# Row-limited scores and a two-queue first stack in the narrow attentions of a four-layer decoder

## The chip, the cores and the metric

The kernel runs on one core of a Trainium2 chip. The metric is the device time of one execution in microseconds, the median of several runs. The profile is of one execution of its own.

## The reference

The input `x` is (4, 512, 128), the context (4, 154, 128). Four layers follow one another, each with a self part, a cross-attention and a feed-forward part, each with its residual and layer norm. What matters here are the six attentions with 16 heads of 8 dimensions, called narrow below: two self-attentions (L0a, L3a) and four cross-attentions over the 154 context rows (L0x, L1x, L2x, L3x; L1x and L3x have masks). Cut to its core, each computes

```
q, k, v = x @ Wq + bq, src @ Wk + bk, src @ Wv + bv       # split into 16 heads of 8
scores  = einsum('bhqd,bhkd->bhqk', q, k) * scale         # the scale is 1 in L0x
y       = softmax(scores) @ v                             # over k, then heads side by side
x       = layernorm(x + y @ Wo + bo)
```

In L0a the source is rotated by cosines and sines first, in L3a it is projected down first. Everything is float32.

## The kernel before

`build` (L3109) runs the stages one after another, each in a block of its own with a barrier behind it: L0a, L0x, a gated feed-forward, four scans (`mamba`), L1x, a mixture of experts, an attention with shared keys, L2x, a convolution with experts, L3a, L3x, a routed feed-forward. Self-attentions are `self_attention` (L203), cross-attentions `cross_attention` (L701). The feed-forward weights of a coming stage are loaded into the tile `stream` by SyncE just ahead of L0x and of L3x.

**Scores with nine terms.** Float32 scores are made of bf16 matmuls. `split_parts` (L193) splits q and k into PARTS = 3 bf16 parts each, with four operations: `qp` and `kp`, 128 rows (64 for each half of eight heads, dimension by head). All nine products of a part of q with a part of k are summed by one matmul whose contraction runs over TERMS * DH = 72 rows (ROWS) of `qs` and `ks`: nine blocks of eight rows. Behind them are PARTS = 3 rows for the parts of the row maxima in `qs`, against ones in `ks`, so that the turned scores (keys on the rows) come out with the maximum subtracted. The matmuls take all 128 rows of both tiles; so `ks` is filled with ones from row 64 on (GpSimd, L482 or L990) and `qs` with zeros (VectorE L537, or VectorE L1046 and GpSimd L991), once a stage. In L0a and L3a `ks` lies in `stream`.

**How the rows come about.** Eight heads at a time (a "half", n = 0 to 7 for four batches). `stack_q` (L651) moves the three parts of q with three transfers into rows 0 to 23 of `qs`; each takes 64 rows of 512 and puts them into 8 rows of 8 x 512. `stack_k` (L661) does so for k. `turn_q` (L668) waits until q's stacks have landed and copies these rows, cyclically shifted, into rows 24 to 71 with four transfers; `turn_k` (L678) copies k's 24 rows twice, unshifted. All of it is issued by SyncE, in this order, and only the semaphore `turned_...` of the six copies releases TensorE. In the cross-attentions these are L1211 to L1245, and k's rows have 154 columns.

**The order of the work** is written out by hand. Each engine walks over steps J from FIRST to LAST, and constants (Q_AT, K_AT, STACK_AT, TURN_AT, ...) say at which J a batch's or a half's piece of work stands. A step holds four matmuls of turned scores (L321, L834), four of scores (L302; in the crosses four pairs, L807) for heads that lie LEAD steps ahead, and the weighing of the values (L335, L850). VectorE reduces every score tile to its maxima (L542, L1052) and ScalarE takes the exponentials (L405, L917). Scores start at J = -LEAD; what comes before is projecting q and k of the first batch (L279, L284; L779, L784), ScalarE's copies of them (L428, L437; L938, L947), the splits of the first batch on VectorE, and the rows of half 0. The splits of the later batches are GpSimd's. `pad_v` (L557, L1067) clears the value tile once a stage: in the self-attentions VectorE does it before the splits of the first batch, in the crosses already behind them. A half is eight heads, so eight steps J of a self-attention and four of a cross-attention. SyncE also issues the rows of maxima (`put_maxima`), in one order with the stacks and copies.

Of the kernel before, what the change touches and what calls it, by code (L numbers as in the profile page):

```python
# [202 lines left out]
def self_attention(k, name, scale, biased=True):  # L203
# [14 lines left out]
    HALVES = 3  # L218
# [13 lines left out]
    with ExitStack() as ctx:  # L232
# [23 lines left out]
        with phase(k, "chain", "pool_chain", "q_proj", "k_proj", "v_proj", "q_sb", "k_sb", "v_sb", "first_parts",  # L256
                   "q_parts", "k_parts", "q_stacked", "k_stacked", "turned_0", "turned_1", "turned_2", "q_cleared", "k_cleared",
                   "src_proj", "src_cos", "src_sin", "src_ready", "scores", "maxed", "split", "mt_ready", "mt_sb", "mt_row_0", "mt_row_1",
                   "scoresT", "exped", "weighed", "z_out", "zt_ready", "zn_ready", "znT_ready", "znT_sb", "y_ready",
                   "y_read", "var_ready", "eps_added", "rstd_ready", "x_ready", "xT_ready", "xT_sb") as (block, s):  # L260
            @block.tensor
            def _(pe):
# [50 lines left out]
                def scores_turned(J, a):  # L313
# [84 lines left out]
            def _(act):  # L398
# [58 lines left out]

                for J in range(FIRST, LAST):
                    for a in range(G):
# [19 lines left out]
            def _(pool):  # L479
# [24 lines left out]
                def q_parts(b, first):  # L504
                    if first:
                        pool.wait_ge(s["q_sb"], b + 1)

                        pool.wait_ge(s["q_stacked"], 16 * PARTS * 2 * b)
# [4 lines left out]
                def k_parts(b):  # L513
                    pool.wait_ge(s["k_sb"], b + 1)
                    pool.wait_ge(s["k_stacked"], 16 * PARTS * 2 * b)
# [18 lines left out]
            def _(dve):  # L534
                chain = Chain(dve, s["chain"])
                for n in range(HALVES):
                    dve.memset(qs[64:P, n].rearrange("p h t -> p (h t)").bitcast(F32), 0.0).then_inc(s["q_cleared"], 1)  # L537
# [77 lines left out]
                for J in range(FIRST, LAST):  # L615
# [6 lines left out]
                    if batch_at(J, Q_AT) == 0:  # L622
                        pad_v()
# [18 lines left out]
            def _(sp):  # L642
# [44 lines left out]
                for J in range(FIRST, LAST):  # L687
                    if group_at(J, TURN_AT + 1) is not None:
                        put_maxima(group_at(J, TURN_AT + 1))
                    if half_at(J, STACK_AT) is not None:  # L690
                        stack_q(half_at(J, STACK_AT))
                    if half_at(J, STACK_AT + 1) is not None:
                        stack_k(half_at(J, STACK_AT + 1))
                    if half_at(J, STACK_AT + 3) is not None:
                        turn_q(half_at(J, STACK_AT + 3))
                    if half_at(J, STACK_AT + 4) is not None:
# [4 lines left out]
def cross_attention(k, name, scale, biased=True, masks=None, scrambled=False):  # L701
# [12 lines left out]
    TURNED, HALF_UNITS = 6 * 16, G * PER_BATCH // 2  # L714
# [14 lines left out]
    with ExitStack() as ctx:  # L729
# [32 lines left out]
        with phase(k, "chain", "pool_chain", "q_proj", "k_proj", "v_proj", "q_sb", "k_sb", "v_sb", "first_parts",  # L762
                   "q_parts", "k_parts", "q_stacked", "k_stacked", "turned_0", "turned_1", "turned_2", "turned_3", "q_cleared", "k_cleared",
                   "masks_in", "mask_q", "mask_k", "scores", "maxed", "split", "mt_ready", "mt_sb", "mt_row_0", "mt_row_1",
                   "scoresT", "exped", "weighed", "z_out", "zt_ready", "zn_ready", "znT_ready", "znT_sb", "y_ready",
                   "biased", "y_read", "var_ready", "eps_added", "rstd_ready", "x_ready", "xT_ready", "xT_sb") as (block, s):
            @block.tensor
            def _(pe):
# [25 lines left out]
                def scores(J, a):  # L794
                    hh, u, i = 2 * (J + LEAD) + a // 2, a % 2, 4 * (J + LEAD) + a
                    b, h = hh // H, hh % H
                    if h % HH == 0 and u == 0:
                        n = hh // HH
                        pe.wait_ge(s[f"turned_{n % 4}"], TURNED * (n // 4 + 1))
# [5 lines left out]
                    for p in range(2):  # L805
                        qt = 2 * u + p
                        last = pe.matmul(ps[:, i % S_RING, 256 * p:256 * p + CTX], qs[:, b % 2, h, qt * P:(qt + 1) * P],  # L807
                                         ks[:, b % 2, h, :], start=p == 0, stop=not masks, skip_group_check=True)
# [14 lines left out]
                def scores_turned(J, a):  # L823
# [10 lines left out]
                    last = pe.matmul(out, ks[:, b % 2, h, t * KV:(t + 1) * KV], qs[:, b % 2, h, :], start=True, stop=not masks)  # L834
# [75 lines left out]
            def _(act):  # L910
# [56 lines left out]

                for J in range(FIRST, LAST):
                    for a in range(G):
# [17 lines left out]
            def _(pool):  # L987
# [3 lines left out]
                pool.memset(qs[64:P, 1].rearrange("p h t -> p (h t)").bitcast(F32), 0.0).then_inc(s["q_cleared"], 1)  # L991
                pool.wait_ge(s["k_cleared"], 2)
                pool.wait_ge(s["q_cleared"], 2)
# [8 lines left out]
                def q_parts(b, first):  # L1002
                    if first:
                        pool.wait_ge(s["q_sb"], b + 1)
                        if b >= 2:

                            for n in range(2 * b - 4, 2 * b - 2):
                                pool.wait_ge(s[f"turned_{n % 4}"], TURNED * (n // 4 + 1))
# [35 lines left out]
            def _(dve):  # L1044
                chain = Chain(dve, s["chain"])
                dve.memset(qs[64:P, 0].rearrange("p h t -> p (h t)").bitcast(F32), 0.0).then_inc(s["q_cleared"], 1)  # L1046
# [143 lines left out]
            def _(sp):  # L1190
# [19 lines left out]

                def stack_q(n):  # L1211
# [16 lines left out]
                def turn_q(n):  # L1228
                    buf, heads = heads_of(n)
                    N = PARTS * DH  # L1230
                    sp.wait_ge(s["q_stacked"], 16 * PARTS * (n + 1))
                    if n == 0:
                        sp.wait_ge(s["q_cleared"], 2)
# [4 lines left out]
                def turn_k(n):  # L1238
                    buf, heads = heads_of(n)
                    N = PARTS * DH  # L1240
                    sp.wait_ge(s["k_stacked"], 16 * PARTS * (n + 1))
                    if n == 0:
# [4 lines left out]
                for J in range(FIRST, LAST):  # L1247
# [4 lines left out]
                    if half_at(J, Q_AT + 3) is not None:  # L1252
                        stack_q(half_at(J, Q_AT + 3))
                    if half_at(J, Q_AT + 4) is not None:
                        stack_k(half_at(J, Q_AT + 4))
                    if half_at(J, Q_AT + 5) is not None:
                        turn_q(half_at(J, Q_AT + 5))
                    if half_at(J, Q_AT + 6) is not None:
# [2146 lines left out]
```

## Time and profile before

| | |
|---|---|
| time, median of 3 runs | 3376.77 us (3366.75 to 3377.44) |
| the profiled execution's own time | 3375.58 us |
| its span, first to last instruction | 3373.6 us |
| TensorE busy | 2740.5 us, 81% of the span |
| VectorE busy | 2080.8 us, 62% |
| ScalarE busy | 1304.8 us, 39% |
| GpSimd busy | 913.2 us, 27% |
| mean granted TensorE clock | 0.904 of 2.4 GHz |
| DMA | 95.04 MB, mean 28 GB/s |

Busy shares are means over the whole span. PE is TensorE, PEld its weight loads, DVE VectorE, ACT ScalarE, POOL GpSimd, SPq the issues of SyncE. The granted clock is a share of 2.4 GHz, so 0.50 is 1.2 GHz.

### The profile page before, as it was taken

How to read it: one execution, taken by the hardware profiler on the slowest of the kernel's cores; microseconds unless marked ns; L12 is line 12 of the kernel's file. 1: busy time of each engine (PE TensorE's matmuls, PEld its weight loads, DVE VectorE, ACT ScalarE, POOL GpSimd, SP SyncE). 2: the span in 40 equal slices, each digit the busy share in tenths (PEclk: the TensorE clock that was granted, in tenths of full speed). 3: DMA queues.
4: the chain of work that ended last, by engine and by line, in shares of the span. 5: the costliest groups of instructions: out<-in, count | busy, mean ns of one | idle time of the engine just before them, and what ended most of it. 6: DMA issues, size and time to landing. Idle time of an engine off the chain costs nothing. (4 is left out here: it accounts for less than half of the span.)

```text
span 3373.6 us, 44323 instructions
## 1 busy us (share of the span) xinstructions
PE 2740.5 (81%) x16400; PEld 1278.7 (38%) x16400; DVE 2080.8 (62%) x4159; ACT 1304.8 (39%) x2241; POOL 913.2 (27%) x1160
## 2 busy tenths in 40 slices
PE   4997869855566598999997999987864799698998
PEld 1332424411121254345554444443432233354555
DVE  5884761287788654566676556556677777463444
ACT  1664543243334254222121434333632466364221
POOL 2101100074475310233341545552135110110000
PEclk9997879977887798999999999997976899798999
DMA  5121300000000220111231000002100320320000
GB/s 130 35 39 44 61 27 1 37 14 0 0 0 0 53 51 4 27 30 37 66 73 44 1 1 1 1 1 50 27 1 3 55 44 16 97 40 1 1 1 13
DMA packets 45494, 95.04 MB, mean 28 GB/s; under 512 B 14168, under 2 KB 33420, under 8 KB 39520
## 3 DMA queue, kind: packets, MB, share of 16 engines
q1 hardware_dynamic: 45280, 92.22, 12.4%
q8 instruction: 131, 2.15, 0.3%
q14 instruction: 83, 0.68, 0.1%
HBM read 46.20 MB, written 1.38 MB: 14 GB/s over the span
## 5 line engine op out<-in xcount | busy, mean ns | idle before, releaser
L1638 POOL TENSOR_TENSOR mamba_dbu<-mamba_du,mamba_b 128x512 f32<-128x512 f32 x128 | 257.0, 2041 | 131.3 <-ACT mamba_b L1621 131.3
L1605 PE MATMUL ps<-mamba_hc,weights 128*128 128x512 f32 x256 | 163.6, 729 | 98.4 <-DVE mamba_hc L1663 97.8
L1652 DVE TENSOR_TENSOR_SCAN mamba_h<-mamba_da,mamba_dbu 128x512 f32<-128x512 f32 x128 | 210.9, 1650 | 18.3 <-ACT mamba_da L1626 18.3
L542 DVE TENSOR_REDUCE L3a_negmax<-ps 128x1 f32<-128x512 f32 x256 | 162.4, 684 | 52.1 <-PE ps L302 51.6
L542 DVE TENSOR_REDUCE L0a_negmax<-ps 128x1 f32<-128x512 f32 x256 | 162.6, 685 | 50.6 <-PE ps L302 50.1
L2438 DVE TENSOR_REDUCE skv_negmax<-ps 128x2 f32<-128x1024 f32 (+3 forms) x128 | 101.2, 799 | 129.4 <-PE ps L2281 129.4
L405 ACT ACTIVATE L0a_probs<-ps 128x512 f32<-128x512 f32 x256 | 143.7, 599 | 77.3 <-PE ps L321 75.6
L405 ACT ACTIVATE L3a_probs<-ps 128x512 f32<-128x512 f32 x256 | 143.7, 599 | 73.4 <-PE ps L321 71.9
L2500 ACT ACTIVATE skv_probs<-ps 128x1024 f32<-128x1024 f32 (+3 forms) x128 | 90.2, 705 | 186.9 <-PE ps L2307 186.9
L164 POOL TENSOR_SCALAR vareps<-mv 128x4 f32<-128x4 f32 x24 | 7.6, 315 | 549.4 <-DVE mv L1279 495.1
L189 PE MATMUL ps<-stream,xT 128*64 128x512 f32 x512 | 129.4, 623 | 14.4 <-DVE moa_v L2063 7.2
L189 PE MATMUL ps<-stream,moa_xm 128*64 128x128 f32 x2048 | 124.9, 275 | 11.6 <-DVE moa_xm L2080 11.1
L189 PEld LDWEIGHTS ps<-stream,moa_xm 128*64 128x64 f32 x2048 | 115.3, 138 | 34.5 <-DVE moa_xm L2080 18.8
L3025 ACT ACTIVATE rffn_sg<-ps 128x512 f32<-128x512 f32 (+1 forms) x96 | 57.0, 596 | 183.7 <-PE ps L2981 183.7
L3069 DVE TENSOR_TENSOR rffn_hid<-rffn_sg,ps 128x512 f32<-128x512 f32 (+1 forms) x96 | 65.2, 685 | 99.7 <-ACT rffn_sg L3025 75.0
L302 PE MATMUL ps<-stream,L3a_qs 128*128 128x512 bf16 x256 | 100.1, 394 | 30.8 <-DMA stream<-stream 17.9
L2450 DVE RECIPROCAL skv_inv<-skv_inv 128x128 f32<-128x128 f32 x128 | 118.0, 934 | 10.1 <-ACT skv_inv L2482 10.1
L302 PE MATMUL ps<-stream,L0a_qs 128*128 128x512 bf16 x256 | 100.5, 395 | 24.4 <-DMA stream<-stream 12.6
L1605 PEld LDWEIGHTS ps<-mamba_hc,weights 128*128 128x128 f32 x256 | 43.9, 210 | 194.1 <-DVE mamba_hc L1663 192.9
L2304 PE MATMUL ps<-skv_qT,skv_kT 64*128 64x256 f32 (+3 forms) x512 | 100.8, 471 | 16.6 <-ACT skv_mt L2518 11.0
L2040 DVE TENSOR_REDUCE moa_negmax<-ps 128x2 f32<-128x256 f32 (+1 forms) x64 | 52.7, 823 | 98.7 <-PE ps L1827 98.6
L189 PE MATMUL ps<-xT,weights 128*64 128x512 f32 x384 | 104.2, 621 | 9.4 <-DVE moa_v L2061 3.5
(619 smaller groups left out, 6586.3 us busy)
## 6 DMA issues: line engine op xcount, KB each, us to landing
moa_masks<-picked SPq DMA_DIRECT2D x32, 512.0 KB, 6.5
stream<-stream SPq DMA_DIRECT2D x32, 192.0 KB
stream<-gate_up_down_in SPq DMA_DIRECT2D x1, 4352.0 KB, 13.0
stream<-value_output_in SPq DMA_DIRECT2D x1, 4096.0 KB, 12.0
moa_gateb<-gates SPq DMA_DIRECT2D x32, 128.0 KB
stream<-ffn_in SPq DMA_DIRECT2D x1, 2888.0 KB, 9.4
L0a_qs<-L0a_qs SPq DMA_DIRECT2D x16, 128.0 KB
L0x_qs<-L0x_qs SPq DMA_DIRECT2D x16, 128.0 KB
```

What stands on the lines that cost most here:

```text
L189: last = pe.matmul(out[at], stationary[:, at], moving, **flags)
L302: pe.matmul(ps[:, i % S_RING, :], qs[:, n % HALVES, h, a * P:(a + 1) * P], ks[:, n % HALVES, h, :], start=True, stop=True).then_inc(s["sco ...
L405: act.activation(probs[:, J % PB, a, :], ps[:, T_BANK + i % T_RING, :], ACT.Exp, scale=scale).then_inc(s["exped"], 1)
L542: dve.tensor_reduce(negmax[:, hh // G % 4, a, hh % G:hh % G + 1], ps[:, i % S_RING, :], AX.X, ALU.max, negate=True).then_inc(s["maxed"], 1)
L1605: pe.matmul(ps[:, 4 + j, :], k.ident, hc[:, (J * n + j) % RING, :], start=n == 0, stop=n == N - 1).then_inc(s["summed"], 1)
L1638: pool.tensor_tensor(dbu[:, i % RING, :], du[:, j, :], bsb[:, n % AHEAD, :], ALU.mult).then_inc(s["dbu_ready"], 1)
L1652: dve.tensor_tensor_scan(out=hs[:, i % RING, :], data0=da[:, i % RING, :], data1=dbu[:, i % RING, :], initial=0.0, op0=ALU.mult, op1=ALU.a ...
L2304: pe.matmul(ps[:, T_BANK + a, q0:], kT[at, r, q0:q0 + P], qT[at, r, q0:], start=True, stop=False)
L2438: dve.tensor_reduce(negmax[:, g % 4, qt, at:at + 2], ps[:, bank:bank + 2, 0:(qt + 1) * P], AX.X, ALU.max, negate=True).then_inc(s["maxed"], 1)
L2450: dve.reciprocal(at, at).then_inc(s["inverted"], 1)
L2500: act.activation(probs[:, step % 2, :, t, t * P:], ps[:, T_BANK:T_BANK + 2, t * P:], ACT.Exp, scale=scale).then_inc(s["exped"], 1)
L3069: dve.tensor_tensor(hid[0:nr, e % 2, t, :], sg[0:nr, i % 2, :], ps[0:nr, 2 * (i % 2) + 1, :], ALU.mult).then_inc(s["hid_ready"], 1)
```

## The change

In both functions:

- The scores' matmuls take rows 0 to 71 of `qs` and `ks`, the turned scores' rows 0 to 74. The clearing of `qs` on VectorE and GpSimd is taken out, with its semaphore; that of `ks` stays.
- Half 0 is no longer stacked and turned. Its nine blocks of q's rows come straight from `qp` by nine transfers that SyncE issues as soon as q's parts are ready (`first_q_rows`), and its nine blocks of k's rows straight from `kp` by nine transfers that ScalarE issues (`first_k_rows`), after k's parts and the ones. All eighteen have the shape of a stack (64 rows into 8). TensorE waits for all of them. Halves 1 to 7 are made as before, and waits are counted anew.
- In the self-attentions `pad_v` moves behind both splits.

The diff of `self_attention`, cut to its core:

```
-                        pe.wait_ge(s[f"turned_{n % HALVES}"], TURNED * (n // HALVES + 1))
+                        pe.wait_ge(*rows_in(n))
...
-                    pe.matmul(ps[:, i % S_RING, :], qs[:, n % HALVES, h, a * P:(a + 1) * P], ks[:, n % HALVES, h, :],
+                    pe.matmul(ps[:, i % S_RING, :], qs[0:ROWS, n % HALVES, h, a * P:(a + 1) * P],
+                              ks[0:ROWS, n % HALVES, h, :],
                               start=True, stop=True).then_inc(s["scores"], 1)
...
-                    pe.matmul(ps[:, T_BANK + i % T_RING, :], ks[:, buf, h, t * P:(t + 1) * P], qs[:, buf, h, :], start=True,
-                              stop=True).then_inc(s["scoresT"], 1)
+                    pe.matmul(ps[:, T_BANK + i % T_RING, :], ks[0:ROWS + PARTS, buf, h, t * P:(t + 1) * P],
+                              qs[0:ROWS + PARTS, buf, h, :], start=True, stop=True).then_inc(s["scoresT"], 1)
...
+                def first_k_rows():
+                    act.wait_ge(s["first_parts"], 2)
+                    act.wait_ge(s["k_cleared"], 1)
+                    for c in range(PARTS):
+                        for r in range(PARTS):
+                            to = DH * (PARTS * r + c)
+                            act.dma_start(ks[to:to + DH, 0, :, :], kp[0:64, c, :]).then_inc(s["first_rows"], 16)
+
                 for J in range(FIRST, LAST):
+                    if half_at(J, STACK_AT) == 0:
+                        first_k_rows()
...
-                for n in range(HALVES):
-                    dve.memset(qs[64:P, n].rearrange("p h t -> p (h t)").bitcast(F32), 0.0).then_inc(s["q_cleared"], 1)
...
                         split_parts(dve, chain, kf[:, :], kp, True, True, s["first_parts"])
-                    if batch_at(J, Q_AT) == 0:
                         pad_v()
...
+                def first_q_rows():
+                    sp.wait_ge(s["first_parts"], 1)
+                    for c in range(PARTS):
+                        for r in range(PARTS):
+                            to = DH * (PARTS * r + (c - r) % PARTS)
+                            sp.dma_start(qs[to:to + DH, 0, :, :], qp[parts_of(0), c, :]).then_inc(s["first_rows"], 16)
+
                 def stack_q(n):
                     b, buf = n // 2, n % HALVES
-                    sp.wait_ge(*((s["first_parts"], 1) if b == 0 else (s["q_parts"], b)))
+                    if b:
+                        sp.wait_ge(s["q_parts"], b)
...
-                    sp.wait_ge(s["q_stacked"], 16 * PARTS * (n + 1))
-                    if n < HALVES:
-                        sp.wait_ge(s["q_cleared"], n + 1)
+                    sp.wait_ge(s["q_stacked"], 16 * PARTS * n)
...
-                    sp.wait_ge(s["k_stacked"], 16 * PARTS * (n + 1))
+                    sp.wait_ge(s["k_stacked"], 16 * PARTS * n)
...
-                    if half_at(J, STACK_AT) is not None:
+                    if half_at(J, STACK_AT) == 0:
+                        first_q_rows()
+                    if half_at(J, STACK_AT):
                         stack_q(half_at(J, STACK_AT))
```

In `cross_attention` the same edits stand with 154 columns for k; the memsets of `qs` that go are L1046 on VectorE and L991 on GpSimd, and `first_k_rows` stands at J = Q_AT + 4, `first_q_rows` at J = Q_AT + 3. GpSimd's splits of later batches wait for `first_rows` where they overwrite the parts.

## Rows read from the trace of the kernel before

**Rows 1.** Busy time by stretches: us, busy by engine (count), granted clock, DMA share, GB/s

```profile
50.00:305.00 255.00, 239.66 (x1276) 76.88 (x1274) 193.60 (x409) 161.40 (x300) 29.75 (x34) 0.99 0.19 33
...
1640.00:2290.00 650.00, 587.92 (x5232) 309.00 (x5228) 399.25 (x575) 208.93 (x326) 298.60 (x559) 0.99 0.09 20
```

**Rows 2.** Groups of instructions by line and shape, TensorE, whole span: busy us, mean ns

```profile
L836 PE MATMUL ps<-L3x_mask_k,bconst 77*77 77x512 bf16 x128 | 48.8, 382 | 0.0
L834 PE MATMUL ps<-L3x_qs,L3x_ks 128*77 128x512 bf16 x128 | 48.7, 380 | 0.0
```

**Rows 3.** Instructions in order of time, start of L0a: start, duration, engine, line [idle]

```profile
25.80 1.09 POOL L486 TENSOR_TENSOR L0a_turned<-xT,weights 128x512 f32<-128x512 f32 x1
...
27.84 1.26 POOL L494 TENSOR_TENSOR L0a_src<-L0a_turned 128x512 f32<-128x512 f32 x1 [0.95 <-DVE L0a_turned L580]
...
31.27 0.69 ACT L428 ACTIVATE L0a_qf<-ps,weights 128x512 f32<-128x512 f32 x1 [9.55 <-PE ps L279]
...
32.34 0.43 DVE L196 CAST L0a_qp<-L0a_qf 128x512 bf16<-128x512 f32 x1
...
34.71 2.18 SPq L658 DMA_DIRECT2D L0a_qs<-L0a_qp  x3
...
36.49 0.69 DVE L200 TENSOR_TENSOR L0a_kp<-L0a_kf,L0a_kp 128x512 bf16<-128x512 f32 x1
...
40.14 2.60 SPq L675 DMA_DIRECT2D L0a_qs<-L0a_qs  x4
...
44.58 2.77 SPq L658 DMA_DIRECT2D L0a_qs<-L0a_qp  x3
...
49.50 1.03 PE L302 MATMUL ps<-stream,L0a_qs 128*128 128x512 bf16 x2 [12.56 <-DMA stream<-stream]
```

**Rows 4.** Instructions in order of time, start of L3a

```profile
2601.79 0.60 ACT L428 ACTIVATE L3a_qf<-ps 128x512 f32<-128x512 f32 x1 [2.23 <-PE ps L279]
...
2604.55 0.60 ACT L437 ACTIVATE L3a_kf<-ps 128x512 f32<-128x512 f32 x1 [2.16 <-PE ps L284]
...
2612.05 0.69 DVE L200 TENSOR_TENSOR L3a_kp<-L3a_kf,L3a_kp 128x512 bf16<-128x512 f32 x1
...
2625.17 1.03 PE L302 MATMUL ps<-stream,L3a_qs 128*128 128x512 bf16 x2 [17.90 <-DMA stream<-stream]
```

**Rows 5.** Instructions in order of time, start of L2x

```profile
2296.53 0.69 ACT L938 ACTIVATE L2x_qf<-ps,weights 128x512 f32<-128x512 f32 x1 [2.75 <-PE ps L779]
...
2298.83 1.50 DVE L196 CAST L2x_qp<-L2x_qf 128x512 bf16<-128x512 f32 x1
...
2302.27 2.08 SPq L1218 DMA_DIRECT2D L2x_qs<-L2x_qp  x3
...
2307.43 2.59 SPq L1235 DMA_DIRECT2D L2x_qs<-L2x_qs  x4
...
2314.39 0.69 PE L807 MATMUL ps<-L2x_ks,L2x_qs 128*128 128x154 bf16 x4 [6.00 <-DMA L2x_ks<-L2x_ks]
...
2316.78 2.56 SPq L1235 DMA_DIRECT2D L2x_qs<-L2x_qs  x4
...
2323.94 0.70 PE L807 MATMUL ps<-L2x_ks,L2x_qs 128*128 128x154 bf16 x4 [0.62 <-DMA L2x_ks<-L2x_ks]
```

**Rows 6.** Instructions in order of time, start of L3x

```profile
2909.08 2.58 SPq L1235 DMA_DIRECT2D L3x_qs<-L3x_qs  x4
...
2915.92 0.44 PE L807 MATMUL ps<-L3x_ks,L3x_qs 128*128 128x154 bf16 x2 [5.88 <-DMA L3x_ks<-L3x_ks]
```

**Rows 7.** Busy time by stretches of one microsecond in L0a, columns as in rows 1

```profile
48.00:49.00 1.00, 0.00 (x0) 0.00 (x0) 0.00 (x0) 0.00 (x0) 0.00 (x0) 1.00 0.58 94
...
50.00:51.00 1.00, 0.64 (x3) 0.10 (x1) 0.85 (x2) 0.00 (x0) 0.00 (x0) 1.00 0.58 68
```

More of the change, by code:

```diff
@@ L260, in self_attention, with rows_in @@
                    "y_read", "var_ready", "eps_added", "rstd_ready", "x_ready", "xT_ready", "xT_sb") as (block, s):
+            def rows_in(n):
+                if n == 0:
+                    return s["first_rows"], FIRST_ROWS
+                return s[f"turned_{n % HALVES}"], TURNED * (n // HALVES + (n % HALVES > 0))
             @block.tensor
@@ L689, in _ @@
                         put_maxima(group_at(J, TURN_AT + 1))
-                    if half_at(J, STACK_AT) is not None:
+                    if half_at(J, STACK_AT) == 0:
+                        first_q_rows()
+                    if half_at(J, STACK_AT):
                         stack_q(half_at(J, STACK_AT))
-                    if half_at(J, STACK_AT + 1) is not None:
+                    if half_at(J, STACK_AT + 1):
                         stack_k(half_at(J, STACK_AT + 1))
-                    if half_at(J, STACK_AT + 3) is not None:
+                    if half_at(J, STACK_AT + 3):
                         turn_q(half_at(J, STACK_AT + 3))
-                    if half_at(J, STACK_AT + 4) is not None:
+                    if half_at(J, STACK_AT + 4):
                         turn_k(half_at(J, STACK_AT + 4))
@@ L766, in cross_attention, with rows_in @@
                    "biased", "y_read", "var_ready", "eps_added", "rstd_ready", "x_ready", "xT_ready", "xT_sb") as (block, s):
+            def rows_in(n):
+                if n == 0:
+                    return s["first_rows"], FIRST_ROWS
+                return s[f"turned_{n % 4}"], TURNED * (n // 4 + (n % 4 > 0))
             @block.tensor
@@ L806, in scores @@
                         qt = 2 * u + p
-                        last = pe.matmul(ps[:, i % S_RING, 256 * p:256 * p + CTX], qs[:, b % 2, h, qt * P:(qt + 1) * P],
-                                         ks[:, b % 2, h, :], start=p == 0, stop=not masks, skip_group_check=True)
+                        last = pe.matmul(ps[:, i % S_RING, 256 * p:256 * p + CTX], qs[0:ROWS, b % 2, h, qt * P:(qt + 1) * P],
+                                         ks[0:ROWS, b % 2, h, :], start=p == 0, stop=not masks, skip_group_check=True)
                     if masks:
@@ L833, in scores_turned @@
                     out = ps[0:KV, T_BANK + i % T_RING, :]
-                    last = pe.matmul(out, ks[:, b % 2, h, t * KV:(t + 1) * KV], qs[:, b % 2, h, :], start=True, stop=not masks)
+                    last = pe.matmul(out, ks[0:ROWS + PARTS, b % 2, h, t * KV:(t + 1) * KV],
+                                     qs[0:ROWS + PARTS, b % 2, h, :], start=True, stop=not masks)
                     if masks:
@@ L966, in copy_x, with first_k_rows @@
                     act.copy(k.xTs[:, b, :], ps[:, B_BANK, :]).then_inc(s["xT_sb"], 1)
+                def first_k_rows():
+                    act.wait_ge(s["first_parts"], 2)
+                    act.wait_ge(s["k_cleared"], 1)
+                    for c in range(PARTS):
+                        for r in range(PARTS):
+                            to = DH * (PARTS * r + c)
+                            act.dma_start(ks[to:to + DH, 0, 0:HH, :], kp[0:64, 0, c, :]).then_inc(s["first_rows"], 16)
                 for J in range(FIRST, LAST):
+                    if half_at(J, Q_AT + 4) == 0:
+                        first_k_rows()
                     for a in range(G):
@@ L1209, in parts_of, with first_q_rows @@
                     return slice(64 * (n % 2), 64 * (n % 2) + 64)
+                def first_q_rows():
+                    sp.wait_ge(s["first_parts"], 1)
+                    for c in range(PARTS):
+                        for r in range(PARTS):
+                            to = DH * (PARTS * r + (c - r) % PARTS)
+                            sp.dma_start(qs[to:to + DH, 0, 0:HH, :], qp[parts_of(0), 0, c, :]).then_inc(s["first_rows"], 16)
                 def stack_q(n):
@@ L1251, in _ @@
                         masks_in(batch_at(J, Q_AT))
-                    if half_at(J, Q_AT + 3) is not None:
+                    if half_at(J, Q_AT + 3) == 0:
+                        first_q_rows()
+                    if half_at(J, Q_AT + 3):
                         stack_q(half_at(J, Q_AT + 3))
-                    if half_at(J, Q_AT + 4) is not None:
+                    if half_at(J, Q_AT + 4):
                         stack_k(half_at(J, Q_AT + 4))
-                    if half_at(J, Q_AT + 5) is not None:
+                    if half_at(J, Q_AT + 5):
                         turn_q(half_at(J, Q_AT + 5))
-                    if half_at(J, Q_AT + 6) is not None:
+                    if half_at(J, Q_AT + 6):
                         turn_k(half_at(J, Q_AT + 6))
```

29 lines of the change are left out of this document (13 added, 16 removed).

## The prediction

> **What bounds the kernel now.** I read the busy time by stretches first [rows 1]. In the first self-attention, once its scores run, TensorE is busy 239.66 of 255.00 us at a granted clock of 0.99: the body of the stage is full, and the change leaves the number and the columns of its matmuls alone. So I went to what the change does touch, the start of each of the six narrow attentions, in order of time. In the first one [rows 3] TensorE sits idle 12.56 us and then starts at 49.50, released by the landing of the last "turned" rows; in the last self-attention [rows 4] the same wait is 17.90 us; in a cross attention [rows 5] it is 6.00 us, with a second, short wait of 0.62 us for the rows of the second eight heads. Nothing covers these waits: VectorE and ScalarE both need the scores. Whatever makes the rows land earlier comes off the end, one for one.
>
> **Part 1, 72 rows for the scores, 75 for the turned ones.** Price nothing. A matmul over 77 rows takes 382 ns where one over 128 rows and equally many columns takes 380 [rows 2]. The stretch of 650 us whose scores have 64 rows is granted 0.99 [rows 1], so fewer rows have not pulled the clock down here.
>
> **Part 2, no clearing, and `pad_v` behind both splits.** In L0a VectorE's three memsets are gone, but GpSimd's for `ks` stay, and its cosine product ends at 25.80 + 1.09 = 26.89. The sum that waited for VectorE until 27.84 can start at 27.0, 0.85 earlier, and with it ScalarE's copy of q ends at 31.1 instead of 31.96. Before, `pad_v` held VectorE until 32.34; now the split follows the copy at once. A split takes 34.69 - 32.34 = 2.35, so q's parts are ready at 33.5 (was 34.7) and k's at 36.3 (was 37.2) [rows 3]. In L3a there is no product, and ScalarE's copies end at 2602.39 and 2605.15: q's parts are ready at 2604.8, k's at 2607.5, where VectorE ended k's at 2612.74 [rows 4]. In a cross attention VectorE's memset kept the first cast waiting until 2298.83 though q was there at 2297.22, and the cast took 1.50 beside GpSimd's memset instead of 0.43 [rows 3, 5]: 1.6 + 1.05 = 2.65 earlier. `pad_v` now comes after k's split (3.5 us, before the values' matmul is read); it is covered by the transfers, at least 10 us long. L0a's second sine moves behind it, to some 40 us, and is needed only after the first scores.
>
> **Part 3, the rows.** Before, SyncE issued 3 + 3 stacks, waited, and issued 4 + 2 turned copies. Now nine q stacks on SyncE and nine k stacks on ScalarE, all of the kind that moves 64 rows into 8. The bytes are the same, but their shape is the slow one. Between 50 and 51 only such stacks are moving and the DMAs move 68 GB/s [rows 7], though SyncE has issued them all by then: 65.5 KB each, so 0.97 us a stack, one after another. Three q stacks issued at 34.71 had landed when the turned copies were issued at 40.14, 5.43 us [rows 3]; in L2x it is 5.16 [rows 5]. Nine therefore land 5.43 + 6 x 0.97 = 11.25 us after their start if the queue is alone.
>
> What two queues move together no row shows, since ScalarE issues no DMA before. The lower end is 68 GB/s for both, the upper 136. In the second from 48 to 49, where turned copies run out as stacks begin, it is 94 [rows 7]; I take 100, next to that row and halfway between the ends. 
> An issue on SyncE takes 2.18 / 3 = 0.73 or 2.08 / 3 = 0.69 [rows 3, 5]. For ScalarE, which has no row, I take the same 0.7. Its bounds: nothing, which gains nothing, as the data take longer than the issues; and 2.77 / 3 = 0.92, SyncE's slowest [rows 3], which hides in the self-attentions (8.3 under 11.8 below) and costs 1.2 us in a cross. Behind these issues on ScalarE stand L3a's copy of `src` and the crosses' copy of q, both of the second batch (in L2x from 2308.2 on); who waits for them is TensorE's next projections and GpSimd's split, needed after the first scores, so they cost nothing unless the issues stretch past 1 us.
>
> L0a: k's data begin 5.43 - 2.91 = 2.5 after 36.3, at 38.8, and 9 x 1.31 = 11.8 later the last row has landed, 50.6. TensorE starts at 50.65 instead of 49.50 [rows 3]: **1.15 lost**. L3a: 2607.5 + 2.5 + 11.8 = 2621.8, against 2625.17 [rows 4]: **3.3 gained**. Their second half has some 24 us of reduces ahead of it, and SyncE is through with its copies by 56.
>
> Crosses: k's stacks are 19.7 KB and one every 0.7 us is 28 GB/s; with q's 68 that is under 100, so q runs alone. q starts at 2302.27 - 2.65 = 2299.6; nine have landed at 2299.6 + 5.16 + 5.8 = 2310.6, k by 2310.4 (a split of at most 2.35, nine issues 6.2, and 5.16 - 2.91 = 2.25 to the landing). The first scores gain 3.7. But the stacks of the second half queue behind the nine: the twelfth lands at 2313.5, and the turned copies that were issued at 2316.78 go out then, 3.2 earlier. That half was already waited for at 2323.94 [rows 5], so it decides: **3.1 gained**, in L0x, L1x and L2x. In L3x the first three stacks land behind the load of the next stage's weights, issued before them on the same queue and not moved by the change, and the copies went out at 2909.08; six more make 2914.9 against 2915.92 [rows 6]: **0.9**.
>
> Sum: -1.15 + 3.3 + 3 x 3.1 + 0.9 = 12.35. The profiled execution took 3375.58 (span 3373.6), so 3363.2; the median of the runs shown is 1.2 above it, so 3364.4.
>
> **Rivals.**
> (a) *Two queues move twice what one does.* For: the second queue writes other rows. Then k in L0a lands at 36.3 + 11.25 = 47.6 (1.9 gained) and in L3a at 2618.8 (6.3 gained), crosses as above: 18.4, 3358.4.
> (b) *Two queues share one queue's rate; slower than before.* For: the 68 GB/s stay flat in row 50:51 with the issues done, so the engines and not the issue are the limit. Then from 38.8 each pair takes 1.95: L0a 56.4 (6.9 lost), L3a 2627.6 (2.4 lost); in the crosses nine k stacks take 9 x 0.29 = 2.6 of q's time, 0.5 gained in three and 1.7 lost in L3x. Sum 9.5 lost, 3386.3. It decides from about 80 GB/s for both down. By the Trainium skill (DMA: Bandwidth & Descriptors, "Issuing engines are not separate DMA queues") all issuers share the same 16 DMA engines and a second one saves only issue time, which is this case. Against it: turned copies have been seen mixed with stacks at 94 [rows 7].
> (c) *The issues of two queues exclude each other.* Eighteen at 0.69 are 12.4 us, and the crosses' last row lands near 2314.4, nothing gained; the selfs as forecast: about 3 gained, 3373.8.
> (d) *Narrow scores lower the clock.* A granted clock of 0.90 for 0.99 would cost 22 us in each self-attention. Against: the 64-row stretch [rows 1].
>
> **How the numbers follow.** Forecast case 0.45, (a) 0.20, (b) 0.20, (c) 0.10, (d) 0.03, others 0.02. About 0.3%, 10 us, is what a measurement of this kernel can tell from no change, and my 12.4 is just past it: of the forecast case I count 0.30 as faster and 0.15 as same. With 0.18 of (a), faster is 0.48; same is 0.15 + 0.02 of (a) + 0.09 of (b) + 0.10 of (c), 0.36; slower is the rest, 0.16. The range goes from just under (a) to (b): 3356 to 3386; the forecast case's own is 3359 to 3371.
>
> **What would show it.** Right: the first scores of L0a within a us or two of 50.6 and later than the parts allow; L3a's 16.7 us after its k copy ends; crosses 3 to 4 us earlier after the stage begins; stretches of 90 to 110 GB/s while both queues have stacks; matmul means of the scores unchanged. Wrong: 68 GB/s there (b), over 120 (a), ScalarE's or SyncE's issues stretched to over 1 us (c), a clock under 0.95 in the body of L0a (d), or a new wait at the second half's rows in a cross that gives all back.

## The result and the profile after

The changed kernel takes **3490.20 us** (median of 6 runs, 3477.47 to 3509.75); the kernel before takes 3370.85 beside it (6 runs, 3366.75 to 3377.44). The ratio is 1.0356 with a 95% interval of 1.0321 to 1.0392: 119 us slower, far outside the range of 3356 to 3386. The profiled execution took 3481.59.

The first view is the page of the changed kernel: busy time by engine, and the granted clock in 40 slices.

```profile
span 3479.7 us, 44350 instructions
...
PE 2873.0 (83%) x16400; PEld 1325.1 (38%) x16400; DVE 2060.9 (59%) x4149; ACT 1307.1 (38%) x2241; POOL 895.3 (26%) x1156
...
PEclk9997658977887688999999999997765699699999
```

The same clock row on the page before:

```profile
PEclk9997879977887798999999999997976899798999
```

TensorE is busy 2873.0 us where it was busy 2740.5, with the same matmuls and columns, while VectorE's and GpSimd's sums fell by the clears (2080.8 to 2060.9, 913.2 to 895.3). The engine itself became slower. The clock row says how: with slices of 87 us (before 84), L0x lies in the fourth to seventh digit, 7658 where it was 787, and L1x and L2x lie lower too. (The 5 in the 31st digit is mostly the convolution stage, which is at 0.67 after and 0.68 before.) The mean granted clock is 0.866 (before 0.904), and it is 0.864 to 0.871 in all six runs.

Next, busy time by stretches, each from the first matmul of a stage to that of the next. The columns are those of [rows 1]. Before, L0x, L1x and L2x:

```profile
320.30:501.10 180.80, 130.93 (x817) 58.17 (x817) 129.93 (x419) 89.57 (x173) 31.00 (x43) 0.75 0.23 51
1129.30:1325.70 196.40, 167.58 (x1121) 87.94 (x1121) 107.74 (x303) 93.47 (x177) 30.44 (x40) 0.88 0.23 46
2294.40:2452.60 158.20, 124.93 (x865) 60.74 (x865) 99.19 (x298) 91.95 (x177) 31.04 (x39) 0.82 0.22 41
```

After: the body of L0a (it answers to the first of [rows 1]), then L0x, L1x, L2x, and 14 us of L0a in which only stacks are moving:

```profile
57.00:336.00 279.00, 260.50 (x1296) 85.64 (x1296) 198.17 (x422) 162.69 (x302) 30.95 (x36) 0.94 0.17 29
336.90:544.70 207.80, 172.71 (x817) 72.51 (x817) 128.34 (x418) 90.26 (x173) 27.43 (x42) 0.57 0.20 44
1178.10:1390.30 212.20, 185.66 (x1120) 95.70 (x1120) 103.74 (x302) 93.84 (x176) 26.90 (x38) 0.80 0.22 43
2355.40:2535.90 180.50, 146.93 (x864) 69.25 (x864) 96.76 (x297) 92.82 (x177) 27.51 (x38) 0.72 0.21 36
36.00:50.00 14.00, 0.00 (x0) 0.00 (x0) 4.33 (x3) 0.00 (x0) 1.26 (x1) 1.00 0.57 64
```

In L0x TensorE runs the same 817 matmuls in 172.71 us instead of 130.93, at 0.57 instead of 0.75; VectorE and GpSimd are busy less than before, ScalarE 0.7 us more. Measured in the same way, the stages grow by 17.5 us (L0a), 27.1 (L0x), 15.8 (L1x), 22.4 (L2x), 13.4 (L3a) and 12.4 (L3x), together 108.6. The mamba stage between L0x and L1x is 6.7 longer and the rest 9.2 shorter, which makes the 106.1 us between the two profiled spans. A closer look at L0x, 40 us from some 100 us into the stage, before and after:

```profile
420.00:460.00 40.00, 35.94 (x246) 15.81 (x244) 33.83 (x120) 27.20 (x52) 2.52 (x4) 0.87 0.11 22
```

```profile
440.00:480.00 40.00, 40.00 (x177) 17.27 (x180) 28.24 (x97) 19.65 (x38) 2.52 (x4) 0.50 0.13 24
480.00:520.00 40.00, 40.00 (x160) 14.53 (x156) 20.84 (x74) 20.61 (x41) 2.51 (x4) 0.50 0.01 2
```

After, the profile shows TensorE without a gap in 80 us, and still it is granted 0.50, 1.2 GHz. Before, with gaps, it was granted 0.87. (The ends of matmuls are modelled in the profile, and at half the clock each takes longer, so the 40.00 is in part a result of the low clock.) By the Trainium skill (TensorE: Matmul & The Clock Gate, "What's actually happening") the clock is set by how busy TensorE has been recently; these rows do not fit that if busy means having a matmul running.

The groups of instructions by line and shape (busy us, mean ns), before and after. L862 answers to L834, L879 to L850, L327 to L321:

```profile
L321 PE MATMUL ps<-L0a_qs,stream 128*128 128x512 bf16 x256 | 96.6, 384 | 1.0 <-ACT L0a_probs L405 0.8
L834 PE MATMUL ps<-L0x_qs,L0x_ks 128*77 128x512 bf16 x128 | 52.7, 431 | 0.3
L850 PE MATMUL ps<-L0x_probs,L0x_v 77*32 77x512 f32 x256 | 38.2, 671 | 0.3 <-ACT L0x_z L955 0.2
```

```profile
L327 PE MATMUL ps<-L0a_qs,stream 75*128 75x512 bf16 x256 | 100.2, 399 | 1.0 <-ACT L0a_probs L411 0.8
L862 PE MATMUL ps<-L0x_qs,L0x_ks 75*77 75x512 bf16 x128 | 69.6, 565 | 0.0
L879 PE MATMUL ps<-L0x_probs,L0x_v 77*32 77x512 f32 x256 | 54.1, 933 | 0.0
```

The last row of each carries most: the weighing matmuls were not touched, 77 rows before and after, and take 933 ns instead of 671. So what is lost is not lost in the narrowed matmuls alone; the others of the stage slow with them.

Last the transfers, in order of time. L0a of the changed kernel, which answers to [rows 3]:

```profile
30.15 0.43 DVE L196 CAST L0a_qp<-L0a_qf 128x512 bf16<-128x512 f32 x1 [7.87 <-ACT L0a_qf L434]
...
32.52 6.07 SPq L671 DMA_DIRECT2D L0a_qs<-L0a_qp  x9
...
35.38 7.19 ACTq L470 DMA_DIRECT2D stream<-L0a_kp  x9
...
38.63 2.10 SPq L681 DMA_DIRECT2D L0a_qs<-L0a_qp  x3
...
56.98 1.04 PE L307 MATMUL ps<-stream,L0a_qs 72*128 72x512 bf16 x2 [21.89 <-DMA stream<-L0a_kp]
```

L3a, which answers to [rows 4], and L2x, which answers to [rows 5]:

```profile
2686.06 0.43 DVE L196 CAST L3a_qp<-L3a_qf 128x512 bf16<-128x512 f32 x1 [8.04 <-ACT L3a_qf L434]
...
2711.82 1.04 PE L307 MATMUL ps<-stream,L3a_qs 72*128 72x512 bf16 x2 [20.91 <-DMA stream<-L3a_kp]
```

```profile
2358.21 0.43 DVE L196 CAST L2x_qp<-L2x_qf 128x512 bf16<-128x512 f32 x1 [5.22 <-ACT L2x_qf L967]
...
2361.72 6.30 ACTq L1003 DMA_DIRECT2D L2x_ks<-L2x_kp  x9
...
2375.79 0.70 PE L835 MATMUL ps<-L2x_ks,L2x_qs 72*128 72x154 bf16 x4 [9.09 <-DMA L2x_ks<-L2x_kp]
```

The first splits start as early as forecast, but the first scores do not. (L0a as a whole begins 1.0 us earlier in this profile, with its first matmul at 19.5 for 20.5.) Counted from the first matmul of the stage: L0a 37.5 us (before 29.0), L3a 31.3 (28.3), L0x 17.6 (19.9), L1x 20.6 (19.9), L2x 20.4 (19.9), L3x 21.4 (22.3). In sum 9.3 us later.

So two losses stand there: some 9 us in the transfers, and the rest in the clock. What causes the clock's fall, the narrow matmuls or the later and rearranged starts, the profile alone doesn't say.

### The profile page after: what moved, and what is told of

It is laid out like the page before. It is cut to its first block and busy times, and to the rows that moved or that the text cites. A ratio compares the mean times of both kernels' runs of the same rounds, so it can differ in the third digit from the quotient of the medians.

```text
span 3479.7 us, 44350 instructions
## 1 busy us (share of the span) xinstructions
PE 2873.0 (83%) x16400; PEld 1325.1 (38%) x16400; DVE 2060.9 (59%) x4149; ACT 1307.1 (38%) x2241; POOL 895.3 (26%) x1156
## 5 line engine op out<-in xcount | busy, mean ns | idle before, releaser
L1648 PE MATMUL ps<-mamba_hc,weights 128*128 128x512 f32 x256 | 172.7, 769 | 94.5 <-DVE mamba_hc L1706 93.9
L307 PE MATMUL ps<-stream,L0a_qs 72*128 72x512 bf16 x256 | 108.3, 427 | 29.4 <-DMA stream<-L0a_kp 21.9
L307 PE MATMUL ps<-stream,L3a_qs 72*128 72x512 bf16 x256 | 107.6, 425 | 28.9 <-DMA stream<-L3a_kp 20.9
L189 PEld LDWEIGHTS ps<-stream,moa_xm 128*64 128x64 f32 x2048 | 116.4, 139 | 33.2 <-DVE moa_xm L2123 18.8
```

Source lines behind the costliest of these rows:

```text
L189: last = pe.matmul(out[at], stationary[:, at], moving, **flags)
L307: pe.matmul(ps[:, i % S_RING, :], qs[0:ROWS, n % HALVES, h, a * P:(a + 1) * P], ks[0:ROWS, n % HALVES, h, :], start=True, stop=True).then_ ...
L1648: pe.matmul(ps[:, 4 + j, :], k.ident, hc[:, (J * n + j) % RING, :], start=n == 0, stop=n == N - 1).then_inc(s["summed"], 1)
```

## The experiments

Every kernel was timed beside runs of the kernel before on the same chip. The differences below are between those medians; the intervals are of the ratio.

### The narrow matmuls alone

```diff
-pe.matmul(ps[:, i % S_RING, :], qs[:, ...], ks[:, ...],
+pe.matmul(ps[:, i % S_RING, :], qs[0:ROWS, ...], ks[0:ROWS, ...],
-pe.matmul(..., ks[:, buf, h, t * P:(t + 1) * P], qs[:, buf, h, :], ...
+pe.matmul(..., ks[0:ROWS + PARTS, buf, h, t * P:(t + 1) * P], qs[0:ROWS + PARTS, buf, h, :], ...
```

(and the same in the cross-attentions)

> The kernel before with one edit: the scores run over 72 rows and the turned scores over 75, while clearing, padding, stacks and turns stay as they were. Theory (fewer contraction rows lower the granted clock): all but the transfers' share of the 119 us comes back, so 90 to 110 us slower than before, 3460 to 3480, mean granted clock 0.865 to 0.875, cold time in the first self-attention above 28 us (21.7 before, 31.6 after) and in the first cross-attention above 150 us (88.6 before, 177.1 after). Rival (the later first scores and the missing clears cause it, the width costs nothing): within 0.3% of before, 3371, clock 0.90.

Measured: 3500.19 (4 runs, 3460.10 to 3505.79), ratio 1.0368 (1.0320 to 1.0415), 132 us slower, clock 0.864. Its L0x (332.20 to 542.30) and L1x by stretches:

```profile
332.20:542.30 210.10, 172.69 (x816) 72.66 (x817) 132.80 (x419) 90.09 (x173) 30.86 (x43) 0.57 0.20 43
1170.70:1412.30 241.60, 215.70 (x1121) 107.29 (x1121) 108.53 (x303) 95.02 (x177) 30.43 (x40) 0.69 0.18 38
```

L0x is that of the changed kernel again, 172.69 us busy at 0.57, though not a transfer or a clear was touched, and its first scores stand at the stage's 19.9 us as before. The rival is out: the width alone costs all that the change costs. The number was 20 us above the top of the expectation. In the profiled run the excess lies in L1x: it grows by 45.1 us at a granted clock of 0.69, where in the changed kernel's profile it grows by 15.8 at 0.80, with the same widths. How far the clock falls in a stage thus differs between narrow kernels, or between executions; the four times of this one spread over 46 us.

### The rest of the change without them

It leaves of the change all but the narrow matmuls, and puts the clears that 128 rows need behind the first splits.

```diff
 # the changed kernel, matmuls over qs[:, ...] and ks[:, ...] again, and on VectorE in a self-attention
+clear(0)
+clear(1)
 # behind both first splits
+clear(2)
 pad_v()
 # in a cross-attention
+dve.memset(qs[64:P, 0, 0:HH] ..., 0.0)
+pool.wait_ge(s["first_parts"], 2)      # then GpSimd clears the rest of qs
```

> The changed kernel's two-queue rows and its late padding, with the matmuls over 128 rows and the clears that they need put off the first splits' way. It leaves of the change all but the narrow matmuls. From the two measured parts (two-queue rows +24, clears and padding late -17): 7 us slower than before, 3371 to 3382, clock 0.90; the narrow matmuls then stand for the other 110 to 115 us of the change. Rival (the parts do not add up, and the change has another cost still): over 25 us slower.

Measured: 3372.10 (11 runs), ratio 1.0009 (1.0000 to 1.0018), 1.9 us slower, clock 0.909. The two parts of it that were also timed singly (below, 24 lost and 17 gained) sum to 7 lost; 1.9 is at the edge of what their intervals allow, and no third cost shows. Of the 119 us of the change some 117 are then the narrow matmuls; alone they cost 132, and the intervals of the two ratios (1.0321 to 1.0392, 1.0320 to 1.0415) overlap.

### What of the width matters: 96 rows, one kind alone, empty rows

```diff
-qs[:, ...], ks[:, ...]
+qs[0:96, ...], ks[0:96, ...]          # both kinds of scores, all six stages
```

> The kernel before with both kinds of scores over 96 rows instead of 128, nothing else. 72 and 75 rows cost 132 us (3500 for 3369, clock 0.864 for 0.905). Theory 1 (each row left out costs alike): 32 of 54 rows, so some 75 us slower, 3445, clock 0.88. Theory 2 (what counts is whether the fourth group of 32 rows is used at all): like 72 rows, 3490 to 3505, clock 0.865. Theory 3 (only the narrowest rows cost): within 15 us of before, 3370 to 3385, clock 0.90.

Measured: 3398.94 (4 runs), ratio 1.0083 (1.0064 to 1.0102), 28.8 us slower, clock 0.889 in the profiled run (0.889 to 0.901 in all four). All three theories miss. The first 32 rows taken away cost 29 us and the next 21 to 24 cost 103 more; nor is the number of 32-row groups in use what counts, since 72, 75 and 96 rows all need three.

The two kinds one at a time, 72 rows for the scores with 128 for the turned ones, and the reverse with 75:

> The kernel before with the scores (first pass, for the maxima) over 72 rows and the turned scores over 128. Both narrow cost 132 us at a mean clock of 0.864. Theory (each kind counts by its busy time, and the two are alike: 97 and 92 us of a self-attention at the fast level, 41 and 50 in a cross): about half, 40 to 90 us slower, clock 0.88 to 0.89. Rival (a threshold: one kind wide is enough to hold the clock): under 30 us slower, clock 0.895 or more.

> The kernel before with the turned scores over 75 rows and the first-pass scores over 128, the mirror of the run beside it. Theory: 40 to 90 us slower, clock 0.88 to 0.89, and this run and its mirror together near the 132 us of both. Rival (a threshold): under 30 us slower each, their sum far below 132.

Measured: 3388.39 (ratio 1.0059, 1.0044 to 1.0074) and 3387.92 (1.0057, 1.0042 to 1.0072), 20 us slower each. Their sum is 40 and both together cost 132. The rival holds: while one kind is wide, the clock mostly holds. By the lengths of the stages in one profile each, the two kinds cost in different places: narrow scores 10.2 us in the two self-attentions and 6.8 in the four crosses, narrow turned scores nothing and 16.8. L0x by stretches, with 96 rows, with narrow scores, with narrow turned scores:

```profile
324.60:521.40 196.80, 155.52 (x817) 66.05 (x817) 131.56 (x419) 90.05 (x173) 30.91 (x43) 0.64 0.21 46
```

```profile
324.40:504.70 180.30, 129.80 (x816) 57.48 (x817) 130.12 (x419) 89.29 (x173) 30.89 (x43) 0.77 0.23 51
```

```profile
318.40:507.90 189.50, 142.02 (x816) 62.15 (x816) 131.03 (x419) 89.73 (x173) 30.87 (x43) 0.70 0.22 48
```

The order of the clocks, 0.77, 0.70, 0.64 and (both narrow) 0.57 against 0.75 before, is that of the stage's lengths. The kernel with narrow turned scores also has the price of a narrow matmul where the clock is up, since in its L0a the stretch from 100 to 300 us is granted 0.99:

```profile
L321 PE MATMUL ps<-L0a_qs,stream 75*128 75x512 bf16 x256 | 96.3, 383 | 3.9 <-ACT L0a_probs L405 1.4 <-issue 1.3 <-DVE L0a_negmax L542 0.5
```

383 ns against the 384 with 128 rows shown above: by itself it costs the same, as forecast.

Then rows that are streamed but hold nothing:

```diff
-pool.memset(ks[64:P, n] ..., TWO_ONES)
+pool.memset(ks[64:96, n] ..., TWO_ONES)
+pool.memset(ks[96:P, n] ..., 0.0)
```

> The kernel before with 128 rows in all scores, but rows 96 to 127 of the k buffers filled with zeros instead of ones, so that both operands are zero there; the zeros take two or three GpSimd clears of 32 rows more at each stage's start, 2 to 5 us a stage at most. Theory (the rows count by being streamed, whatever they hold): clock 0.90, 0 to 20 us slower than before. Rival (rows count by what they hold): the clock falls towards 0.87 to 0.88 and the time by 50 us or more.

Measured: 3375.12 (10 runs), ratio 1.0014 (1.0004 to 1.0023), 4.9 us slower, clock 0.905 in the profiled run. Its L0x:

```profile
326.70:509.10 182.40, 131.21 (x816) 57.93 (x816) 130.47 (x419) 89.35 (x173) 33.45 (x45) 0.76 0.23 50
```

Zero times zero in 32 rows holds the clock as well as ones times zero, while the same 32 rows left out cost 28.8 us. So what counts is that the matmul runs over the rows, not what they hold. (Both operands have them, the one loaded as weights and the one streamed; no run separates the two.) The 5 us fit L0a, where GpSimd's three more clears stand ahead of its cosine product: its first scores come 33.2 us into the stage for 29.0, and the stage is 5.3 us longer. L0x is 1.8 longer, L1x 2.9 shorter, the others within 0.3.

### Is a cold clock handed on?

The narrow widths in L0a and L3a only.

> The kernel before with 72 and 75 rows in the two self-attentions alone, 128 in the four cross-attentions. By the stage lengths of the kernel with all of them narrow, the self-attentions' own loss is 11.5 and 8.4 us, so the theory that each stage pays for its own matmuls gives 20 to 30 us slower, 3390 to 3400. Rival (the clock's state is handed on, and the first cross-attention pays for the self-attention ahead of it): 40 us or more slower, with over 15 of them in the cross-attentions, cold time in the first one above 110 us for 88.6.

Measured: 3396.33 (4 runs, 3386.57 to 3402.32), ratio 1.0076 (1.0052 to 1.0101), 28.3 us slower. L0a is 311.1 us long (before 299.8), L3a 309.3 (296.7), L0x 180.9 (180.7), L1x 196.4 (196.4):

```profile
330.60:511.40 180.80, 130.95 (x816) 57.98 (x816) 129.95 (x419) 89.46 (x172) 30.87 (x43) 0.75 0.23 51
```

That is the L0x of before, to 0.02 us of TensorE's busy time. Each stage pays for its own matmuls, and the first theory holds. The rest of the 132 us, about 100, is then the four crosses'. And narrowing costs where the clock was high too: L0a's body was granted 0.99 before [rows 1].

### Two queues against one

The new rows with everything else as before: 128 rows, the clears ahead of the splits. First by two queues (the transfers of the change, with a wait for `q_cleared` ahead of q's), then from that kernel to one where SyncE issues all eighteen stacks:

```diff
                 for J in range(FIRST, LAST):
-                    if half_at(J, STACK_AT) == 0:
-                        first_k_rows()
...
                     if half_at(J, STACK_AT) == 0:
                         first_q_rows()
+                        first_k_rows()
```

> The new transfers alone: the first half's 18 stacks straight from the parts, q by SyncE and k by ScalarE, but the matmuls over all 128 rows and the clearing and the padding kept ahead of the splits as before. Theory (width lowers the clock, transfers cost by the shared rate of 65 to 69 GB/s): clock 0.90, 10 to 25 us slower than before (L0a's first scores at 57 to 58 for 49.5, L3a's 5 to 8 later in the stage than before since the clearing stays too, crosses 0 to 4 later each). Rival (the transfers are what upsets the clock): more than 60 us slower, clock below 0.88.

> The transfers of the two-queue kernel with full width, but all 18 stacks issued by SyncE, q's nine and then k's nine, so one queue moves them. Theory (two queues share one rate, 64 KB a us): the 18th stack lands 18 us after the first, as with two queues; issuing takes 12 us and hides behind the landings, so the first scores are within 1.5 us of the two-queue kernel's in every stage and the time is within 0.3% of it. Rival (two queues do move more): the first scores 3 us or more later in each of the six stages, 15 to 20 us slower than with two queues.

Measured: 3392.28 us with two queues (5 runs, ratio 1.0078, 1.0065 to 1.0090, clock 0.903), 3392.68 with one (5 runs, ratio 1.0073, 1.0058 to 1.0089, clock 0.899). The same time. Both are 24 us slower than before, at the upper end of what was expected. Ten microseconds of L0a in which only stacks move, with two queues, and with one:

```profile
44.00:54.00 10.00, 0.00 (x0) 0.00 (x0) 0.00 (x0) 0.00 (x0) 0.00 (x0) 1.00 0.57 68
```

```profile
42.00:52.00 10.00, 0.00 (x0) 0.00 (x0) 0.00 (x0) 0.00 (x0) 0.00 (x0) 1.00 0.57 67
```

68 GB/s and 67: the second queue moves nothing more. The start of L0a with two queues, and with one:

```profile
34.70 6.13 SPq L675 DMA_DIRECT2D L0a_qs<-L0a_qp  x9
...
37.21 6.92 ACTq L470 DMA_DIRECT2D stream<-L0a_kp  x9
...
40.88 2.16 SPq L685 DMA_DIRECT2D L0a_qs<-L0a_qp  x3
...
57.51 1.03 PE L307 MATMUL ps<-stream,L0a_qs 128*128 128x512 bf16 x2 [20.58 <-DMA stream<-L0a_kp]
```

```profile
34.18 6.09 SPq L673 DMA_DIRECT2D L0a_qs<-L0a_qp  x9
...
40.38 5.82 SPq L665 DMA_DIRECT2D stream<-L0a_kp  x9
46.25 1.91 SPq L683 DMA_DIRECT2D L0a_qs<-L0a_qp  x3
...
54.35 1.03 PE L307 MATMUL ps<-stream,L0a_qs 128*128 128x512 bf16 x2 [17.94 <-DMA stream<-L0a_kp]
```

From the first issue to the first scores it takes 22.81 us with two queues and 20.17 with one. The expectation put them within 1.5 us; one queue is in fact the quicker by 2.6 here, by 2.5 in L3a and by 1.6 to 2.0 in the first three crosses (counted from the stage's start), and the slower by 2.7 only in L3x. The rows suggest why: with two queues SyncE goes on at 40.88 with the stacks of the second half, and these take turns with k's first ones on ScalarE's queue; with one queue they stand behind them, at 46.25. Three stacks at 0.97 us [rows 7] are about the difference. That this is the cause is argued from the order in the rows and was not tried by itself. Over the six stages the first scores are 8.0 us earlier with one queue, yet in the total no difference shows; why is open.

### The clears out of the way, nothing else

The kernel before with its stacks, turned copies and 128 rows; the clears and `pad_v` moved as in the second experiment.

> The kernel before, with its stacks, turns and 128 rows, but the clears and the padding off the way of the first splits: in a self-attention VectorE clears two of three buffers ahead and the third and pads V after the splits; in a cross-attention VectorE clears the first eight heads only and GpSimd the rest behind the first splits. Theory: the first q split starts 5.3 earlier in L3a, up to 1.1 in L0a, 1 to 3 in each of three crosses, and the first scores move with it since stacks and turns are unchanged; 8 to 15 us faster than before, about 3358, clock 0.90. Rival (the start is bound by the transfers or by the projections whatever the splits do, or GpSimd's clears beside VectorE's work slow both): within 0.1% of before.

Measured: **3351.49** (5 runs, 3347.58 to 3356.62), ratio 0.9952 (0.9938 to 0.9965), 17 us faster than before, clock 0.908. Its L3a:

```profile
2586.12 0.43 DVE L196 CAST L3a_qp<-L3a_qf 128x512 bf16<-128x512 f32 x1 [1.17 <-ACT L3a_qf L428]
...
2591.71 1.76 DVE L537 MEMSET L3a_qs<- 64x2048 f32 x1 [0.48 <-issue]
...
2603.54 0.63 PE L302 MATMUL ps<-stream,L3a_qs 128*128 128x512 bf16 x1 [12.56 <-DMA stream<-stream]
```

The first scores stand 22.9 us into the stage instead of 28.3 (5.3 earlier); in L0a they are 1.3 earlier, in three crosses 2.6 to 2.7, in L3x 0.9 later: 13.8 earlier in sum. This is the one useful part of the change, and it needs neither narrow matmuls nor new transfers.

### More rows than before

If rows hold the clock up, the other narrow matmuls of the crosses should help too:

```diff
-last = pe.matmul(ps[...], v[0:KV, ...], probs[0:KV, ...], ...)
+last = pe.matmul(ps[...], v[:, ...], probs[:, ...], ...)
-last = pe.matmul(out, wb(k, "ident")[0:KV, 0:KV], mask_k[:, b % 2, t, :], ...)
+last = pe.matmul(out, wb(k, "ident")[:, 0:KV], mask_k[:, b % 2, t, :], ...)
 # once a stage, behind pad_v
+dve.memset(probs[64:P, ...], 0.0)
+dve.memset(mask_k[64:P, ...], 0.0)
```

> The kernel with late clears (3351.5), and in the cross-attentions the 256 weighing matmuls and the 128 mask_k matmuls of a stage over 128 rows instead of 77, the rows above 77 padded with zeros once a stage (3.5 us on VectorE while it is idle). The computation is the same. Theory (more rows keep the clock up): cold time in the first cross-attention below 74 us and in the others below 44, 53 and 37, 10 to 40 us faster, 3310 to 3340, clock above 0.91. Rival (these matmuls are too small a part, or what counts is another thing that the scores alone had): within 5 us of 3351.5.

Measured: 3352.13 (5 runs, ratio 0.9941, 0.9928 to 0.9955), 18.1 us faster than before where the kernel with late clears alone was 17.1 faster: no difference. The theory fails on the time. The clock did rise a little in the crosses (L0x 0.81 for 0.79, L1x 0.91 for 0.89, L2x 0.85 for 0.83), but the three stages together became 4.6 us shorter (by their stretches) in profiled runs that differ by as much in stages that nobody touched:

```profile
316.80:492.60 175.80, 124.80 (x817) 55.17 (x817) 130.64 (x420) 89.16 (x173) 32.73 (x44) 0.81 0.24 52
```

TensorE is busy 124.80 of 175.80 us here, VectorE 130.64: a faster clock may have little left to shorten, though no run shows that this is the reason.

## Why the prediction was wrong, point by point

**Part 1, priced at nothing: the step that failed.** "Fewer rows have not pulled the clock down here" was read from one stretch, 650 us with 64-row scores at 0.99 [rows 1]. That stretch is not what it was taken for. Its groups of instructions, 64-row and 128-row ones:

```profile
L189 PE MATMUL ps<-stream,moa_xm 128*64 128x128 f32 x1280 | 77.4, 274 | 8.1 <-DVE moa_xm L2080 7.7
L189 PE MATMUL ps<-xT,weights 128*64 128x512 f32 x280 | 76.9, 628 | 5.9 <-ACT skv_qT L2506 3.4 <-PEq L3174 2.5
L2281 PE MATMUL ps<-bconst 64*128 64x128 bf16 x512 | 35.6, 216 | 0.0
L2277 PE MATMUL ps<-skv_kT,skv_qT 64*128 64x512 f32 x128 | 33.7, 604 | 0.0
```

Its 64-row scores stand among matmuls over 128 rows, which are six of its nine largest groups (the first two here are the largest), and the runs with one narrow kind show that the clock mostly holds while the other kind is wide. It differs in the operands too: its scores are of 32-bit ones at some 600 ns for 512 columns, where the narrow attentions run bf16 matmuls of 380 to 400 ns. (It is no denser than L0a's body: TensorE is busy 587.92 of its 650 us, 90%, and 239.66 of 255 us there, 94%.) One stretch that held the clock said nothing of another kind of stretch, and the crosses' own rows, at 0.75, 0.88 and 0.82 before in L0x, L1x and L2x, do not enter the prediction: there the clock was already down for part of the time. Which of the differences protects the stretch was not tried. What the runs showed in place of "price nothing": the two widths alone cost 132 us, at a mean clock of 0.864. The other half of the step, that a narrow matmul costs the same by itself, was right (383 for 384 ns). Rival (d) named the mechanism and "a clock under 0.95 in the body of L0a" as its sign, which came (0.94). It got 0.03 on the strength of that same stretch, and was priced at 22 us in each self-attention and at nothing in the crosses. Narrowing the two self-attentions alone cost 28 us; about 100 fell in the crosses.

**Part 2, the splits.** Right. In L0a q's split starts 10.6 us into the stage, which is the forecast (31.1 less the 20.5 of the stage's start), in L3a 5.5 us into it (before 11.3), and in a cross the first cast takes 0.43 instead of 1.50. Alone it is worth 17 us, where the first scores account for 13.8; the forecast hid it in one sum with the new rows.

**Part 3, two queues at 100 GB/s.** Mis-sized: 68. In the stretches of nothing but stacks the two queues move 64 to 68 GB/s, as one alone does, and one queue is as fast. The row of 94 GB/s [rows 7] was a mixture of two kinds of transfer, and no reason to go above the flat 68 beside it. Rival (b) had the mechanism. That its numbers came so near, L0a's first scores at 56.4 (56.98 came) and 9.5 us lost in all (9.3 by the first scores), is partly luck: L0a began 1.0 us earlier in the profile after, so that (b) should have had 55.4 there, and by stages it is off, with 0.5 gained in each of three crosses and 1.7 lost in L3x where 2.3 were gained in L0x, 0.6 and 0.4 lost in L1x and L2x, and 0.9 gained in L3x. Neither (b) nor the forecast lets k's nine share the rate with the stacks of the second half, which in L0a are issued from 38.63 on, before k's nine are all issued. By the Trainium skill (SBUF — State Buffer, "Door 1: The DMA port swizzle") the rate depends on how many ports the rows reach; that two queues into different rows could nearly double was the prediction's own step from it, and no run shows a gain. By the Trainium skill (DMA: Bandwidth & Descriptors, "Issuing engines are not separate DMA queues") a second issuer saves only issue time, and here the runs agree: 68 GB/s with two queues, 67 with one.

**Rival (c)** fell: ScalarE's nine issues take 6.30 to 7.19 us, 0.70 to 0.80 each, while SyncE's nine take 6.07 beside them in L0a.

**The crosses' second half**, whose later rows were to leave 3.1 us of gain, did not decide in L1x and L2x: the first scores had no gain to hand on there.

With the clock left out, the change is worth 1.9 us lost (the second experiment), where the forecast had 12.35 gained and rival (b) 9.5 lost. The sum of the new rows (24 lost) and the late clears (17 gained) is 7.

## What to carry to other kernels

Don't narrow a contraction to save reads or clears in bf16 stages like these without reading the clock: 53 to 56 rows that added nothing to a matmul's time held it up, and without them the other matmuls of the stage were slower too, in L0x the untouched weighing ones most (933 ns for 671). Read the granted clock stage by stage, and take a counter-example only from a stage that has the same kind of matmul and no other. A second issuing queue is no second bandwidth: where one queue's transfers already run back to back, look for fewer bytes, another shape, or an earlier start. Of these only the last was tried: moving the clears behind the first splits gave 0.5% for a few moved lines.

## What the runs showed of the hardware that was not expected

- TensorE busy 80.00 us out of 80 was granted 0.50 throughout (L0x of the changed kernel, 440 to 520), while 40 us of the same stage with 128-row scores, busy for 35.94, were granted 0.87.
- The number of contraction rows moves the granted clock, and not in proportion: 128 rows 0.904, 96 rows 0.889, 72 and 75 rows 0.864 (profiled runs); one kind at 72 or 75 costs 20 us, the other 20, both 132.
- 32 rows that hold zeros on both sides hold the clock as well as others (0.905, against 0.889 without them).
- The narrow kernels scatter more: 3460 to 3506 and 3477 to 3510, against 3362 to 3370 for the kernel before in nine runs beside the first of them.
- Stacks of 64 rows into 8 share 64 to 68 GB/s, at a DMA share of 0.57, however many queues issue them.
